# Relative-position products with the table as the stationary operand, written key by query without a copy and a turn, and the first head's maxima spread over the value tiles

## What is computed

```python
qkv = x @ w_qkv + b_qkv                       # heads of 32 channels
attn = jnp.einsum('bnd,bmd->bnm', q * scale, k)
# Rh[y, ky] = rel_pos_h[y - ky + 31], Rw[x, kx] = rel_pos_w[x - kx + 31]
rel_h = jnp.einsum('bhwc,hkc->bhwk', r_q, Rh)
rel_w = jnp.einsum('bhwc,wkc->bhwk', r_q, Rw)
attn = attn.reshape(Bn, q_h, q_w, k_h, k_w)
attn = attn + rel_h[..., :, None] + rel_w[..., None, :]
attn = jax.nn.softmax(attn.astype(jnp.float32), axis=-1)
out = attn @ v
```

## Time and profile before

| | |
|---|---|
| median of 3 runs | 649.78 us (648.08 to 650.61) |
| the profiled execution | 647.42 us |
| its span, first to last instruction | 645.6 us |
| mean granted TensorE clock | 0.984 |
| PE busy, records | 608.9 us (94%), x4473 |
| DVE busy | 394.6 us (61%) |
| ACT busy | 300.7 us (47%) |
| POOL busy | 172.0 us (27%) |

### The profile page before, as it was taken

One profiled execution on the slowest core, in us unless ns is written; L12 is line 12 of the kernel. 1 busy time (PEld: TensorE's weight loads), 2 busy tenths in 40 slices (PEclk: granted clock), 3 DMA queues, 4 the chain that ended last, 5 costly groups with the idle time before them and its releaser, 6 DMA issues.

```text
span 645.6 us, 11986 instructions
## 1 busy us (share of the span) xinstructions
PE 608.9 (94%) x4473; PEld 505.7 (78%) x4473; DVE 394.6 (61%) x664; ACT 300.7 (47%) x419; POOL 172.0 (27%) x106
## 2 busy tenths in 40 slices
PE   3998999999999999999976999999999999999996
PEld 3876866665656655656865899999999999999994
DVE  7567676556566566662478887547654675557635
ACT  4654335444444444446164544444543554354523
POOL 1300076556775555776600000000000000000000
PEclk9999999999999999999986999999999999999998
DMA  8045054442234443100250442434444433443302
GB/s 263 2 82 124 1 123 83 83 84 58 45 60 81 81 81 65 54 0 2 99 183 1 129 160 83 165 125 151 144 147 147 146 119 118 149 164 110 111 1 98
DMA packets 37410, 63.33 MB, mean 98 GB/s; under 512 B 3864, under 2 KB 32894, under 8 KB 37246
## 3 DMA queue, kind: packets, MB, share of 16 engines
q1 hardware_dynamic: 37374, 62.83, 34.6%
HBM read 44.16 MB, written 1.57 MB: 71 GB/s over the span
## 4 chain that ended last, share of the span: by engine, by line
PE 84%; DVE 9%; ACT 2%; POOL 2%; issue 1%; DMA 1%; SPq 1%; POOLq 0%; DVEq 0%
PE ps L747 20%; PE ps L763 20%; PE ps L551 11%; PE ps L560 9%; PE ps L537 8%; PE ps L461 6%; DVE rhalf L1113 5%; POOL acc L395 2%; PE ps L491 1%; PE ps L718 1%; PE ps L773 1%; PE ps L581 1%; DMA onehot<-c_onehot 1%; PE ps L446 1%; PE ps L780 1%
## 5 line engine op out<-in xcount | busy, mean ns | idle before, releaser
L1113 DVE TENSOR_REDUCE rhalf<-ps 128x1 f32<-128x512 f32 x192 | 128.6, 689 | 62.8 <-PE ps L537 62.6
L906 ACT ACTIVATE prob<-ps 128x1024 f32<-128x1024 f32 x96 | 96.8, 1026 | 106.8 <-PE ps L551 106.8
L395 POOL TENSOR_TENSOR acc<-acc,prob 128x1024 f32<-128x1024 f32 x48 | 115.3, 2403 | 6.0 <-ACT prob L906 2.1
L551 PE MATMUL ps<-qst,kst 128*128 128x512 f32 x384 | 108.6, 397 | 0.0
L747 PE MATMUL ps<-xeh,wih 128*128 128x320 f32 (+1 forms) x288 | 89.9, 312 | 1.0 <-ACT xeh L968 1.0
L537 PE MATMUL ps<-kst,qst 128*128 128x512 f32 x192 | 84.2, 442 | 7.0 <-DVE rhalf L1113 3.2
L763 PE MATMUL ps<-hh,woh 128*128 128x320 f32 x288 | 89.4, 310 | 0.0
L763 PE MATMUL ps<-hl,woh 128*128 128x320 f32 x288 | 89.2, 310 | 0.0
L747 PE MATMUL ps<-xel,wih 128*128 128x320 f32 (+1 forms) x288 | 89.2, 310 | 0.0
L747 PE MATMUL ps<-xeh,wil 128*128 128x320 f32 (+1 forms) x288 | 89.1, 309 | 0.0
L763 PE MATMUL ps<-hh,wol 128*128 128x320 f32 x288 | 89.1, 309 | 0.0
(11 more groups left out here) (157 smaller groups left out, 927.3 us busy)
## 6 DMA issues: line engine op xcount, KB each, us to landing
raw_i<-in_L_ffn_wi SPq DMA_DIRECT2D x32, 576.0 KB, 4.9
raw_o<-in_L_ffn_wo SPq DMA_DIRECT2D x32, 576.0 KB, 4.0
xs<-in_x SPq DMA_DIRECT2D x8, 384.0 KB, 4.6
qst<-qh SPq DMA_DIRECT2D x12, 256.0 KB, 3.1
qst<-relh SPq DMA_DIRECT2D x12, 256.0 KB, 3.9
qst<-relw SPq DMA_DIRECT2D x12, 256.0 KB, 4.5
kst<-kp SPq DMA_DIRECT2D x12, 256.0 KB, 5.2
qst<-ql SPq DMA_DIRECT2D x12, 128.0 KB, 3.1
```

Of the source, the lines that this page charges most:

```text
L395: nc.gpsimd.tensor_tensor(acc[:, :], acc[:, :], prob[:, t % SLOT, :], ALU.add).then_inc(sum_add, 1)
L551: last = mm(bank(2 * (t % 2) + half), kst[b][:, part, t * P:(t + 1) * P], qst[b][:, part, half * BANK:(half + 1) * BANK], start=part == 0, ...
L906: run(prob[:, t % SLOT, :], ps[:, 2 * (t % 2) * BANK:2 * (t % 2 + 1) * BANK], ACT.Exp).then_inc(exp_done, 1)
L1113: ve.tensor_reduce(rhalf[:, p // 2, p % 2:p % 2 + 1], bank(4 + p % 2), AX_X, ALU.max).then_inc(max_red, 1)
```

## The change

The position product has its operands exchanged: a block of the table for one head (128 by 32) is the stationary operand, and the 32 queries are the moving operand. The result stands key by query, as the next step wants it. So the copy to `rst`, the four transposes and their two semaphores go. There are now 64 products of 32 moving columns in a term, in place of 16 of 128, and the terms rotate over four banks (0 to 3). For kind 1 the moving queries are 128 bytes apart and the results are written 64 bytes apart in the bank; ACT and DVE then write `relw` in runs of 16 neighbours. Of the first head's maxima, eight stand behind the terms 5, 7, 9 and 11 (two each) and eight behind the value tiles 0 to 3 (two each); `turn_max` and `negate_max` follow value tile 4 in place of tile 1. Value tiles 0 to 2 each wait for the one term whose bank they take.

```diff
--- before.py
+++ after.py
@@ -106,7 +106,6 @@
     rel = [new(n, [P, 2, DC, T], F32R) for n in ("relh", "relw")]
     v0 = room(TD)
     vt = place("vt", [P, NT, D], F32, v0)
-    rst = place("rst", [P, 2, BANK], F32, v0)
     onehot = place("onehot", [P, T], F32, v0 + 8 * BANK)
 
     q0, q1 = room(16 * T), room(16 * T)
@@ -190,8 +189,7 @@
         turned, turn_act, turn_dve = sem("turned"), sem("turn_act"), sem("turn_dve")
         proj_mm, q_act, hi_act, lo_dve, v_mm, v_dve = (
             sem(n) for n in ("proj_mm", "q_act", "hi_act", "lo_dve", "v_mm", "v_dve"))
-        rel_products_mm, rel_copied, rel_mm, rel_act, rel_dve = (
-            sem(n) for n in ("rel_products_mm", "rel_copied", "rel_mm", "rel_act", "rel_dve"))
+        rel_mm, rel_act, rel_dve = (sem(n) for n in ("rel_mm", "rel_act", "rel_dve"))
 
         heads_in = [sem(f"heads_in{b}") for b in range(3)]
         vh_ready, max_mm, max_red, max_whole, max_turned, mneg_ready, mrow_in = (
@@ -232,6 +230,7 @@
         QK_BANKS = [6, 7, 4, 5]
 
         REL = [(kind, c, half) for c in range(DC) for kind in range(2) for half in range(2)]
+        REL_BANKS = 4
         V_BANKS = [0, 1, 2, 6]
 
         X_TURNS = [0, 1, 2, 3, 4, 5]
@@ -264,11 +263,11 @@
 
 
             kind, c, half = REL[n]
-            b, w = bank(2 + n % 2), SIDE // 2
+            b, w = bank(n % REL_BANKS), SIDE // 2
             if kind == 0:
                 return rel[0][:, part, c, half * BANK:(half + 1) * BANK], b
-            return (rel[1][:, part, c, :].rearrange("p (r w) -> p w r", w=SIDE)[:, half * w:(half + 1) * w, :],
-                    b.rearrange("p (w r) -> p w r", w=w))
+            return (rel[1][:, part, c, :].rearrange("p (r w) -> p r w", w=SIDE)[:, :, half * w:(half + 1) * w],
+                    b.rearrange("p (r w) -> p r w", w=w))
 
 
         @block.sync
@@ -483,31 +482,22 @@
 
 
                 kind, c, half = REL[n]
-                wait(pe, rel_copied, n - 1)
-                for t in range(HALF):
+                wait(pe, rel_dve, n - REL_BANKS + 1)
+                out_bank = bank(n % REL_BANKS)
+                for i in range(SIDE // 2):
+                    r = half * SIDE // 2 + i
+                    cols = slice(i * SIDE, (i + 1) * SIDE) if kind == 0 else slice(i, BANK, SIDE // 2)
+                    q_of_r = qf[:, c, r * SIDE:(r + 1) * SIDE] if kind == 0 else qf[:, c, r:T:SIDE]
                     for j in range(HPG):
-                        r = (half * HALF + t) * HPG + j
-                        q_of_r = qf[:, c, r * SIDE:(r + 1) * SIDE] if kind == 0 else qf[:, c, r:T:SIDE]
-                        last = mm(bank(n % 2)[j * SIDE:(j + 1) * SIDE, t * P:(t + 1) * P], q_of_r,
-                                  bd[:, kind, :, SIDE - 1 - r:2 * SIDE - 1 - r], start=True, stop=True)
-                last.then_inc(rel_products_mm, 1)
-
-            def rel_turn(n):
-                pe.wait_ge(rel_copied, n + 1)
-                wait(pe, rel_dve, n - 1)
-                for t in range(HALF):
-                    last = nc.tensor.transpose(bank(2 + n % 2)[:, t * P:(t + 1) * P],
-                                               rst[:, n % 2, t * P:(t + 1) * P], ident[:, :])
+                        last = mm(out_bank[j * SIDE:(j + 1) * SIDE, cols],
+                                  bd[:, kind, j, SIDE - 1 - r:2 * SIDE - 1 - r], q_of_r, start=True, stop=True)
                 last.then_inc(rel_mm, 1)
 
             def rel_terms(first, end, between):
                 pe.wait_ge(q_act, end // 2)
                 for n in range(first, end):
                     rel_products(n)
-                    if n > first:
-                        rel_turn(n - 1)
                     between(n)
-                rel_turn(end - 1)
 
             for n in range(4):
                 qk(n)
@@ -517,8 +507,8 @@
 
             def value_tile(t):
                 wait(pe, v_dve, t - 3)
-                if t == 2:
-                    pe.wait_ge(rel_dve, 4 * DC)
+                if t < 3:
+                    pe.wait_ge(rel_dve, 4 * DC - REL_BANKS + t + 1)
                 for c in range(DC):
                     last = three(bank(V_BANKS[t % 4], D), [x_[:, c, t * P:(t + 1) * P] for x_ in (xnh, xnl)],
                                  [w[:, c, :] for w in (wvh, wvl)], c == 0, c == DC - 1)
@@ -630,18 +620,22 @@
 
             def first_max(n):
 
-                if n == 4:
+                if n == 5:
                     pe.wait_ge(lo_dve, 4 * DC)
                     pe.wait_ge(rows_set, 2)
                     pe.wait_ge(k_rows, 1)
-                for p in range(2 * (n - 4), 2 * (n - 3)):
-                    max_scores(0, 0, 0, p)
+                if n % 2:
+                    for p in range(n - 5, n - 3):
+                        max_scores(0, 0, 0, p)
 
             rel_terms(4, 4 * DC, first_max)
             pe.wait_ge(w_lo, 2 * DC + 1)
             for t in range(NT):
                 value_tile(t)
-                if t == 1:
+                if t < HALF:
+                    for p in range(NT + 2 * t, NT + 2 * t + 2):
+                        max_scores(0, 0, 0, p)
+                if t == HALF:
                     turn_max(0)
             pe.wait_ge(v_dve, NT - 2)
             pe.wait_ge(rows_set, 3)
@@ -877,12 +871,7 @@
             def rels(first, end):
 
                 for n in range(first, end):
-                    act.wait_ge(rel_products_mm, n + 1)
-                    wait(act, rel_mm, n - 1)
-                    run(rst[:, n % 2, :], bank(n % 2), ACT.Copy).then_inc(rel_copied, 1)
-                    if n > first:
-                        rel_high(n - 1)
-                rel_high(end - 1)
+                    rel_high(n)
 
             units(0, 4)
             rels(0, 4)
@@ -1142,14 +1131,19 @@
                 negate_max(h + 1)
 
             for n in range(4, 4 * DC):
-                reduce_max(0, 2 * (n - 4))
-                reduce_max(0, 2 * (n - 4) + 1)
+                if n % 2:
+                    reduce_max(0, n - 5)
+                    reduce_max(0, n - 4)
                 rel_low(n)
-            whole_max(0)
             for t in range(NT):
                 dve.wait_ge(v_mm, t + 1)
                 ve.tensor_tensor(vt[:, t, :], bank(V_BANKS[t % 4], D), bv[:, :], ALU.add).then_inc(v_dve, 1)
-                if t == 1:
+                if t < HALF:
+                    reduce_max(0, NT + 2 * t)
+                    reduce_max(0, NT + 2 * t + 1)
+                if t == HALF - 1:
+                    whole_max(0)
+                if t == HALF:
                     negate_max(0)
             head(0, first=True)
             with dve.Fori(1, NH - 1) as h:
```

## The result

The changed kernel is slower. Its median is 668.54 us (664.86 to 671.82, 4 runs) against 649.76 (648.08 to 650.61, 4 runs) for the kernel before: ratio 1.0292, 95% interval 1.0266 to 1.0319. The profiled execution has a span of 666.0 us (645.6 before) and a mean granted clock of 0.969. The forecast was 643.0.

The account below looks back on a forecast made before the run. Ahead of head 0, PE in a round with ACT and DVE was taken to bound the terms. Terms 0 to 3 gain 1.4 us, terms 4 to 11 with value tiles 5.5; 649.8 - 6.9 gives 643.0 us, range 638 to 659.

Parts of the forecast that it names:

- the value tiles: Value stage ahead of head 0: PE bounds it at 14.5 us, with eight maxima at 0.23 us each.
- the evictions of `relw`: Kind 1's high and low parts, written in runs of 16, fall from 1.10 and 1.16 us to `relh`'s price, 0.69 on DVE.
- The wait for the transfer of the maxima: After value tile 4: 2.9 us are left for 4 KB to land, so it was costed at nothing.
- the bounds of x: x is one position term's stream on PE: 0.87 us if only columns count, 3.49 if groups of four cost as now.
- instruction-bound rival: Position terms: PE limited by issuing 256 records a term; 658.8 us at 80 ns a group, 670.0 at 109; chance 0.30.
- x = 0.96: Kind 0's position terms: 30 ns for each group of four products, making a term's stream on PE 0.96 us.
- 13.6 ns a record: Fastest sustained PE issue shown by the old trace's position products: 8 records in 109 ns.
- x = 1.50: Kind 1's position terms, queries 128 bytes apart: 47 ns a group, chosen between 27 or 30 and 78, 1.50 us a term.
- 51 ns more: Kind 1's strided query reads: upper cost for 32 elements, from weight loads of 159 ns against 108 for rows.
- the prediction's own formula: Whole change: gain = 21.7 - 12x, mean x 1.23, gain 6.9 us, nothing gained from x = 1.81 on.
- That clock: Position terms: a clock below full, where it was full before, was named as a cause not priced.
- 666.5 us: Position terms by the skill's rule of 25 ns between matmul starts: 3.2 us a term, a loss of 16.7.

Follow-up runs that it names:

- run 4: The kernel before with only its first-head maxima spread as in the change: 647.84 us, ratio 0.9972.
- run 2: The changed kernel with kind 1 reading its queries and writing its results side by side, without strides: 669.98 us, ratio 1.0314.
- run 6: The changed kernel with the second half of each term's products left out, 128 records fetched and executed per term: 645.12 us, ratio 0.9935.
- run 3: The kernel before with each position product of 128 columns cut in four of 32, 256 records a term: 680.93 us, ratio 1.0503.
- run 5: The changed kernel with each term replaced by two hardware-loop passes over its first 128 records: 655.30 us, ratio 1.0103.
- run 7: The changed kernel with its terms spread singly ahead of query and key units and value tiles, maxima around tiles 0 to 3: 658.25 us, ratio 1.0145.
- run 8: The kernel of run 7 with column-table terms free of both the strided read and the strided write: 652.27 us, ratio 1.0058.
- run 9: The kernel of run 7 with column-table queries read plain, writes still at a stride: 650.09 us, ratio 1.0017.
- run 10: The kernel of run 7 with column-table results written side by side and the bank read turned, queries still strided: 657.41 us, ratio 1.0141.
- run 11: Complete kernel against the one before: row-table terms by new products, column-table terms by old ones with copy and turn, all spread: 648.65 us, ratio 0.9982.
- run 1: The changed kernel with each term's 64 products issued from a hardware loop over its first eight: 668.09 us, ratio 1.0295.

## Why the prediction was wrong

*What bounds the kernel:* right, and so were the value tiles (14.8 us for 14.5) and the evictions of `relw` (688 ns on DVE for an assumed 692). The wait for the transfer of the maxima did not come. The spread maxima alone are worth 1.8 us by the medians beside run 4 (649.67 to 647.84).

*The step that failed* is the one after the bounds of x: "So the queue can start four pairs in 30 ns, and the 109 ns between groups are the 128 columns themselves." It takes a burst of 30 ns for a rate that lasts 256 records. The first half of its own argument is even right: with instructions at hand and plain reads a group of four costs (1.23 - 0.14) / 32 = 34 ns, for the 30 assumed. What it leaves out is where the instructions come from. The text names this doubt in the instruction-bound rival ("may come out of a filled queue") and then gives it 0.30, because it looked for a limit on PE's pace. The limit is no pace: PE ran at full rate and stopped, up to 2.2 us at a time, and 256 records took 3.5 us where x = 0.96 was forecast. That rival foretold an even pace above 7 ns in both kinds, and its price of 670.0 for a group of 109 ns lies near the result by a mechanism that the trace does not show. That its 13.6 ns a record is nearly the 13.5 of the fetch is luck: the one was read from groups of 128 columns, the other is a page.

*The second miss is a size.* Kind 1 was put at 47 ns a group, x = 1.50, with 78 ns as its upper end. It took (3.00 - 0.14) / 32 = 89 ns, x = 2.86. The choice rested on the idea that one moving stream reads easier than four loads; it reads dearer. The upper bound, 51 ns more, came from weight loads, and a bound from another operation was none.

*The sum by the prediction's own formula.* With x at 1.09 and 2.86 the mean is 1.98, and 21.7 - 12 x 1.98 = -2.0: the strides alone turn the gain of 6.9 into a loss of 2.0, about 652 us. Terms 0 to 3 by the same terms are 2 x 1.09 + 2 x 2.86 + 0.25 = 8.2 us; with the stops that the chain lists (2.24, 1.74, 0.42) 12.6, measured 13.0. Terms 4 to 11 are 4 x (1.09 + 2.86) + 4 x 0.95 = 19.6; with their stops (8.5 in all) 28.1, measured 29.6. The 1.9 us that remain are left for the half clock, which I have not measured apart; 0.5 of them are the two maxima at 77.61, which took 1.15 us where two take 0.66 at full clock. That clock was named as unpriced. What brings it on stays open: runs 2 and 6 have it in this stage and runs 3, 5 and 7 to 11 have not, but run 1 has it without a stop, and runs 8, 9 and 11 have stops of 1.7 to 1.8 us without it.

*Why one experiment misled.* The two causes cover each other. While the fetch is the limit, a page takes 3.5 us and a column term of 3.0 hides in it: taking the strides away gave nothing in the changed kernel (run 2) and 8 us in the spread one (run 9). Spreading gave 10 us with the strides and, with them gone, the kernel is level with the one before. From 668.5 us, 10.3 go with the spreading (run 7; 9.1 us of stops leave the chain, and the half clock), 8.2 to the strided reads (run 9), and what is left is level with before, not faster. By the sum, x = 1.09 in both kinds should gain 8.6 us; run 9 still has 5.7 us of stops, but that these are what is missing is argued, not shown.

*The rules of the Trainium skill.* "SBUF — State Buffer", section "Door 1: The DMA port swizzle", was right against my choice in its first half: strided reads cost, here 55 ns a group. Its second half, that a non-contiguous PSUM pattern slows matmuls, is not seen in 32 columns 64 bytes apart (runs 7 and 10, 39 products in 0.6 us in both; in run 9, which has that write and plain reads, 95). "TensorE: Matmul & The Clock Gate", section "Wait — 56ns, not 53.3ns?", gave 666.5 us, close to the result and again by no mechanism of this trace: without a stop the 128 products of a row term take 1.09 us, 8.5 ns each, over four quarters. On the fetch, "Runtime: NRT & Kernel Launch" says in its section "Instruction fetch mechanics" that the engine takes in blocks of 16 KB, 256 instructions, and that the fetch hides behind the pace of the issue. The packets of 16 KB for 253 records agree; that the fetch is hidden does not hold here, since PE runs a term of 256 records in 1.23 us.

*Still open:* why more than 1 us passes before a page's packet starts and again behind it, and whether the stop could be shorter with the pages placed otherwise.

## What to carry to other kernels

Count instructions not only per engine but per page: unrolled code of very short matmuls is bound by its fetch (here 13.5 ns a record, 108 ns for four products with their loads, where these took 34 with the records at hand), long before the columns bind it, and "issue" gaps at even distances with a packet of the instruction queue for each are its sign. Put such code singly between long matmuls, so that the next page comes in under them, and weigh what it saves there: here a term with copy and turn took 1.68 us where it was spread, against 1.23 for the new one. And when an ablation gives nothing, ask whether another limit was covering it before calling the thing free; repeat it where that limit is gone.

## What the hardware showed that I had not expected

- Short fp32 products over four quarters start every 8.5 ns on average, each with its load; a row term of 128 products and 128 loads takes 1.23 us to its end.
- 256 such records outrun their fetch: nine stops of 0.4 to 2.2 us, 12.9 us in all, one packet of 16 KB for 253 records. A page takes 3.5 us, of which its packet takes about 1, and 4.3 to 4.5 beside 200 GB/s of other transfers.
- Reading 32 fp32 columns 128 bytes apart as the moving operand costs 55 ns for four products, 3.00 us a term against 1.23; writing them 64 bytes apart costs nothing.
- A hardware loop over 32 short records starts a pass every 0.45 us (run 1), where its four groups stream in 0.14: some 0.3 us a pass, of which 0.12 show as a gap. Run 5 has the same 0.3 with passes of 128.
- Cut in four and issued four in a row to the same quarter, with the queries loaded as weights, the products of a row term take 2.7 us; in the changed kernel's order, quarters in turn, 1.23. Order and operands were not told apart.
